# A CIN tower on one core: one-hot products turned round, and tile 1's gathers held until they are done

## The reference, cut to what matters

```python
e = jnp.stack([tbl_0[ids[:, 0]], ..., tbl_23[ids[:, 23]]], axis=1)   # 1024 x 24 x 16
for W in Ws:                                                         # three layers, 64 maps each
    Wr = W.reshape(24, H_prev, 64)
    Xk = jnp.einsum('bfd,bhd,fho->bod', X0, Xk, Wr)
    outs.append(Xk.sum(axis=2))
h = jnp.concatenate([z, dense_ctx], axis=1)
h = jnp.maximum(h @ W_top1 + b_top1, 0.0)
h = jnp.maximum(h @ W_top2 + b_top2, 0.0)
y = h @ W_top3
```

## Time and profile before

| what | value |
|---|---|
| median of 3 runs (lowest, highest) | 413.58 us (409.85, 417.03) |
| the profiled execution, in all | 417.16 us |
| its span, first to last instruction | 415.3 us |
| PE / VectorE / ScalarE / POOL busy | 87% / 73% / 44% / 56% of the span |
| mean granted TensorE clock | 0.992 |

### The profile page before, as it was taken

One profiled execution on the slowest core, in us unless ns is written; L12 is line 12 of the kernel. 1 busy time (PEld: TensorE's weight loads), 2 busy tenths in 40 slices (PEclk: granted clock), 3 DMA queues, 4 the chain that ended last, 5 costly groups with the idle time before them and its releaser, 6 DMA issues.

```text
span 415.3 us, 6926 instructions
## 1 busy us (share of the span) xinstructions
PE 363.0 (87%) x2624; PEld 161.1 (39%) x2624; DVE 302.4 (73%) x299; ACT 184.6 (44%) x347; POOL 231.3 (56%) x324
## 2 busy tenths in 40 slices
PE   1531485999999999898999999999899999999997
PEld 0200372523323333344343434444343354443465
DVE  3210452599698989859798989989799999898700
ACT  1000110024362426444756566565457475745374
POOL 5777106888888888888878888888830000000000
PEclk9999998899999999999999999999999999999999
DMA  7520047969988798998799989997999899941000
GB/s 217 154 42 6 2 96 170 243 134 230 209 214 208 178 242 153 235 243 196 155 227 244 240 162 228 257 253 145 234 252 261 156 238 239 225 117 36 2 1 4
DMA packets 56884, 71.07 MB, mean 171 GB/s; under 512 B 31153, under 2 KB 36017, under 8 KB 56850
## 3 DMA queue, kind: packets, MB, share of 16 engines
q1 hardware_dynamic: 49138, 69.04, 71.7%
q0 software_dynamic: 5632, 1.45, 3.4%
q10 hardware_dynamic: 2080, 0.13, 0.3%
HBM read 50.15 MB, written 1.58 MB: 125 GB/s over the span
## 4 chain that ended last, share of the span: by engine, by line
PE 80%; issue 9%; DMA 4%; ACT 3%; DVE 2%; another core or an unknown queue 2%; SPq 0%; DVEq 0%; ACTq 0%
PE ps_x L406 48%; PE ps_b L406 12%; PE ps_tower L406 9%; PE ps_turn L406 6%; PE ps_turn L459 2%; DMA x_scratch<-x_rows 1%; PE ps_turn L467 1%; DMA small_ids_sb<-small_ids 1%; DVE Z L383 1%; DMA C<-x_scratch 1%; PE ps_tower L412 1%; DVE Z L373 1%; ACT x_diag L691 1%; ACT C L665 0%
## 5 line engine op out<-in xcount | busy, mean ns | idle before, releaser
L383 DVE TENSOR_TENSOR Z<-A,ps_b 128x1024 f32<-128x1024 f32 x192 | 221.8, 1213 | 18.9 <-PE ps_x L406 13.6
L215 POOL DMA_INDIRECT x_rows<-tbl,ids_sb x176 | 180.4, 1025 | 52.7 <-issue 23.9
L406 PE MATMUL ps_x<-Z,w_sb 128*64 128x512 f32 x768 | 184.9, 598 | 0.9 <-DVE Z L383 0.5
L406 PEld LDWEIGHTS ps_x<-Z,w_sb 128*64 128x64 f32 x768 | 49.4, 136 | 80.8 <-issue 58.9
L373 DVE TENSOR_TENSOR Z<-A,C 128x1024 f32<-128x1024 f32 x48 | 57.4, 1222 | 30.5 <-DMA C<-x_scratch 10.4
L227 POOL MEMSET pause_sb<- 128x288 f32 x144 | 50.7, 352 | 21.4 <-DMA x_scratch<-x_rows 21.3
L691 ACT ACTIVATE x_diag<-ps_turn,mask_sb 128x192 f32<-128x192 f32 x128 | 50.6, 605 | 12.2 <-PE ps_turn L467 11.6
L406 PE MATMUL ps_b<-Z,small_sb 128*16 128x128 f32 x288 | 21.1, 357 | 34.7 <-issue 25.2
L406 PE MATMUL ps_x<-Z,w0s_sb 128*64 128x512 f32 x192 | 46.3, 608 | 5.5 <-DVE Z L373 5.3
L704 ACT COPY G<-ps_turn 128x416 f32<-128x416 f32 x31 | 15.7, 506 | 61.4 <-PE ps_turn L406 42.8
L674 ACT COPY ps_b<-B_sb 128x1024 f32<-128x1024 f32 x36 | 37.1, 1030 | 0.0
(11 more groups left out here) (60 smaller groups left out, 192.7 us busy)
## 6 DMA issues: line engine op xcount, KB each, us to landing
A<-x_scratch SPq DMA_DIRECT2D x48, 512.0 KB
B_sb<-x_sb SPq DMA_DIRECT2D x72, 256.0 KB
C<-x_scratch SPq DMA_DIRECT2D x32, 512.0 KB
x_rows<-tbl,ids_sb POOLq DMA_INDIRECT x176
x_quarters<-x_scratch SPq DMA_DIRECT2D x16, 96.0 KB
x_scratch<-x_rows SPq DMA_DIRECT2D x7, 192.0 KB
small_ids_sb<-small_ids SPq DMA_DIRECT2D x2, 512.0 KB, 5.2
w_sb<-w SPq DMA_DIRECT2D x2, 384.0 KB
```

What stands on the lines that cost most here:

```text
L215: pool.indirect_dma_start(out=x0_rows[t % 2][:, f * D:(f + 1) * D], out_offset=None, in_=tables[f], in_offset=bass.IndirectOffsetOnAxis(ap ...
L383: nc.vector.tensor_tensor(Z[s % ZR][:, :], A[u % AS][i][:, :], ps_b[j % 2][:, :], ALU.mult)\
L406: return nc.tensor.matmul(out, lhsT, rhs, start=start, stop=stop)
```

## The change

In the products the operands change places: the ones (128 x 128) are held in the array and the table's chunk (128 x 16) streams. A product's result is then one sample a partition and 16 numbers wide, so the eight tables of a set stand side by side in the first 128 columns of one bank of `ps_b`, and ScalarE copies them straight into `x0_rows`. `x0_small`, its two memsets, its eight copies and the four transposes go. All products of a set are one accumulation in that bank: the first clears it, the last ends it. The wait for the identity moves behind the products. POOL waits, between tile 0's eight gathers and tile 1's 24, until all 18 chunks have been used.

```diff
@@ POOL
             for f in range(FR):
                 gather(0, f, first_gathered)
+            pool.wait_ge(hot_used, len(HOT))
             for t in range(1, TILES):
@@ VectorE
-            for k in range(SETS):
-                nc.vector.memset(x0_small[k][:, :], 0.0).then_inc(small_ids_ready, 1)
             dve.wait_ge(small_rows_in, 16)
...
-                    dve.wait_ge(small_ids_ready, SETS + k + 1)
+                    dve.wait_ge(small_ids_ready, k + 1)
@@ TensorE
-            def turn_small(k):
-                pe.wait_ge(ident_in, 16)
-                pe.wait_ge(small_copied, 4 * (k + 1))
-                for half in range(2):
-                    last = nc.tensor.transpose((ps_turn, ps_x2)[k][:, TILE_ROWS * half:TILE_ROWS * (half + 1)],
-                                               x0_small[k][:, TILE_ROWS * half:TILE_ROWS * (half + 1)], id_sb[:, :])
-                last.then_inc(small_turned, 1)
...
                 pe.wait_ge(hot_ready, n + 1)
                 for f in range(FR):
-                    g, half = f % 4, f // 4
-                    last = mm(ps_b[k][32 * g:32 * g + D, 512 * half:512 * half + TILE_ROWS], small_sb[:, n, f, :],
-                              Z[n % ZR][0:CR, TILE_ROWS * f:TILE_ROWS * (f + 1)], c == 0, c == chunks[k] - 1)
+
+                    last = mm(ps_b[k][:, D * f:D * (f + 1)], Z[n % ZR][0:CR, TILE_ROWS * f:TILE_ROWS * (f + 1)],
+                              small_sb[:, n, f, :], (c, f) == (0, 0), (c, f) == (chunks[k] - 1, FR - 1))
                 last.then_inc(hot_used, 1)
-                if c == 2 and k > 0:
-                    turn_small(0)
-            turn_small(SETS - 1)
+            pe.wait_ge(ident_in, 16)
             keep_warm(WARM[0])
@@ ScalarE
-            act.wait_ge(small_ids_ready, SETS)
             for k in range(SETS):
                 act.wait_ge(hot_used, sum(chunks[:k + 1]))
-                for g in range(4):
-                    nc.scalar.copy(x0_small[k][32 * g:32 * g + D, :].rearrange("p (h b) -> p h b", h=2),
-                                   ps_b[k][32 * g:32 * g + D, :].rearrange("p (h b) -> p h b", h=2)[:, :, 0:TILE_ROWS])\
-                        .then_inc(small_copied, 1)
-                act.wait_ge(small_turned, k + 1)
-                nc.scalar.copy(x0_rows[0][:, FR * D * (k + 1):FR * D * (k + 2)].rearrange("p (f d) -> p f d", d=D),
-                               (ps_turn, ps_x2)[k][:, 0:2 * TILE_ROWS].rearrange("p (f e) -> p f e", e=32)[:, :, 0:D])\
+                nc.scalar.copy(x0_rows[0][:, FR * D * (k + 1):FR * D * (k + 2)], ps_b[k][:, 0:FR * D])\
                     .then_inc(small_ready, 1)
```

More of the change, by code:

```diff
@@ L95, in cin_tower @@
         small_ids_f32 = [sb(f"small_ids_f32_{k}", [CR, FR * TILE_ROWS]) for k in range(SETS)]
-        x0_small = [sb(f"x0_small{k}", [128, 2 * TILE_ROWS]) for k in range(SETS)]
         pause_sb = sb("pause_sb", [128, PAUSE])
@@ L157, in cin_tower @@
         paused = sem("paused")
-        hot_used, small_turned = sem("hot_used"), sem("small_turned")
+        hot_used = sem("hot_used")
         z_used, b_made, x2_turned, x0_turned, g_summed = (sem(n) for n in (
@@ L164, in cin_tower @@
             "z3_summed", "h1_summed", "h2_summed", "y_summed"))
-        small_copied, small_ready = sem("small_copied"), sem("small_ready")
+        small_ready = sem("small_ready")
         c_copied, b_copied = sem("c_copied"), sem("b_copied")
```

## The result

The changed kernel takes 459.8 us, the median of four runs (446.12 to 470.18), beside 413.05 us (409.85 to 417.03). The ratio is 1.089 (95% interval 1.0702 to 1.1078); like every ratio here it compares fast runs alone, 446.12 us and a fifth run of 451.15 us with some 412 us, since the other three of the four (457.99 us and more) were slow runs. By the medians the kernel is slower by 47 us, by the ratio by 37 us, where the forecast had it 10 us faster, and both lie outside the range, which ended at 432 us.

The account below looks back on a forecast made before the run. Bound: a late, serial start behind slow one-hot products, then POOL's gather chain. Of 26 us gained at the start, 7.5 us slack plus 2.5 us earlier chain, 10 us, are kept: 417.16 to 407, from the median 404 us; range 400 to 432.

Parts of the forecast that it names:

- A pair of 128 + 16 is 64 ns fast and 131 ns slow.: Turned products on PE: weight load plus stream, costed per column at 0.44 ns fast and 0.91 ns slow.
- The slow pace for the first 4.7 us and the fast one for 252.: PE clock during the products: 36 pairs slow in 4.7 us, then 252 pairs fast in 16.1 us.
- rival 1: Products keep the slow pace, 288 x 131 ns, ending at 47 to 49 us; kernel 418 us; chance 0.22.
- Products end at 32 us.: End of the one-hot products on PE: 9.3 + 4.7 + 16.1 + 2 = 32 us, where they ended at 56.2.
- I take the slow stretch as gone: PE's sparse products from 14 to 47 us vanish once tile 1's gathers wait; 2 us remain for the first eight gathers.
- 2.4 us of copies and transposes go.: Between last product and store issue: 2.4 us before, about 0.6 us remaining, 1.8 us gained.
- It lands 6.1 us later: Tile 0's store, issued at 32.6 us, lands at 38.7 us, 26 us earlier than before.
- Tile 1's gathers take 30 us.: POOL: 24 gathers x 1.26 us from 32 us, leaving POOL free at 62.3 us against 64.79 before.
- Slack 7.5 us.: Tile 7's chain from last gather to use: 4 us before the use plus 3.5 us of SP held before the store.
- Rival 2: Gathers slow the keep-warm transposes and first cross product instead; gain 3 us, 410.5 us; chance 0.14.
- Rival 3: Slow stretch is not the gathers' doing; products end near 64 us, POOL stands still, kernel 436 us; chance 0.22.
- The rule of the Trainium skill: PE weight load takes columns divided by 1.2 in ns, 107 for 128; products would end near 46 us.

Follow-up runs that it names:

- the wide kernel: Changed kernel with each product streaming all eight tables, 128 columns instead of 16, into the same 128 columns; 428.14 us.
- the paced kernel: Kernel before with the 288-column pause memset before each of tile 1's gathers too; 396.66 us beside 415.69, later 395.6 us, ratio 1.0173.
- the fourth group: Runs without a crawl: kernel before 389.76 us, changed kernel 446.35, pause for tile 1 395.6, kernel before with the wait alone 397.69.

## Why the prediction was wrong, step by step

- *"A pair of 128 + 16 is 64 ns fast and 131 ns slow."* The step that failed. I split the transpose's 113 ns evenly over 256 columns. But load and stream overlap: the wide kernel's pair takes 111 ns at the fast clock with 128 streamed columns, a pair with 16 takes 103. The load alone sets the pair. Measured: 103 ns at 2.4 GHz, 212 ns at 1.2 GHz. The bound of 233 ns, the slow transpose, was the nearest row, and I took half of it.
- *"The slow pace for the first 4.7 us and the fast one for 252."* Failed too. The clock never rose in 61.6 us of pairs. I had seen it rise behind products of 128 streamed columns and carried that to 16. "A stream of pairs without a gap is as dense as PE gets", my argument against rival 1, is what the forced clock in the kernel with 40 more transposes refutes.
- *Products end at 32 us.* It should have been 9.3 + 288 x 0.213 = 70.6; measured 70.9. Of the 38.9 us of error 11.4 are the price of the pair (22 pairs in 4.7 us, then 266 x 0.103 us, and the 2 us for the gathers, would have ended at 43.4 us), and the other 27.5 the clock.
- *"I take the slow stretch as gone" beside the products.* Right: not one gap. But it was not gone from the kernel. With the old products the wait only moved it behind them.
- *2.4 us of copies and transposes go.* Right, or better: the store is issued 0.3 us behind the last product. *It lands 6.1 us later*: SP's load follows after 2.2 us here, and after 2.3 us in the kernel before where it doesn't crawl, but after 5.1 us in the paced kernel of the same group. What the longer ones wait for is not shown.
- *Tile 1's gathers take 30 us.* 33.3 us to the pause, since some take 1.9 us or more. POOL is free at 104.4 instead of 62.3 us: 38.9 + 3.2.
- *Slack 7.5 us.* Behind tile 2's first gather lay 349.8 us before, and 339.2 after: 10.6 us. My split of tile 7's chain came near it by luck: its 3.5 us for SP are 2.7 by the rows that it names (10.3 less 7.6), and the reason was another. These 10 us were no room in the transfers. In the kernel before, the crawl had made the compute late, and by these numbers the compute set the end, with 337.9 us behind the copy of x1, much as in four experiments where x1 comes late too (332.7 to 336.3 us); POOL's chain had the rest to spare. Where the crawl is missing, x1 is copied at 43.3 us, 339.0 us lie behind tile 2's first gather, and the slack is zero.
- *Rival 1* has the right mechanism (16 streamed columns may not raise the clock, or the load is slower than I cost it) and the wrong size, 131 for 212 ns: it put the end at 47 to 49 us and the time at 418. With the lateness that was measured, 39.6 us for tile 2's chain, less its 7.5 of slack, its sum gives 32 us on top of the profiled 417.16: 449.3 against 446.12 measured. *Rival 2* is what the wait alone does. *Rival 3* named the right rule ("a gap later than that costs POOL's chain its full length") and the wrong cause.
- *The rule of the Trainium skill* ("TensorE: Matmul & The Clock Gate", "LDWEIGHTS"), 107 ns for a load, I set aside because a pair with 128 more columns took 113. I had written the exception (the two overlap) and not given it a sum of its own. At the fast clock it holds (103 ns), and at the slow one the measured load takes twice that (212 ns).

The sum above is for the profiled execution. It took 446.12 us, no more than the fourth group's 444.54 to 448.13 us, where the changed kernel has no crawl: the 4.25 us steps at 102 to 107 us cost its end nothing that can be measured. Why three others of the median took 457.99 to 470.18 us is not shown, since none of them has a profile. In two other kernels with the wait, the one with 128 streamed columns and the one with 40 more transposes, 349.5 and 349.9 us lie behind tile 2's first gather where 339.2 do here, so some 10 us can be lost behind the wait. The kernel meant to take such a loss away, wait and pause together, ran in a group without the crawl.

**What stays open.** Why tile 1's gathers slow the issue of PE and VectorE in four groups of runs (that of the result is one) and not in two. By the times of the kernel before it is all or nothing within a group, the kernels and the data are the same, and one chip number has shown both. That the gathers bring it is shown (it comes, moves and goes with them); what else must be there is not. That PE ran short of instructions because their own loads were slowed was not tested.

## What to carry to other kernels

Before operands change places, price the pair by its dearer half: with 128 columns held and 16 streamed, the load is the whole price, and the clock that such a stream gets is to be read from a stream of the same shape, not from a dense one of another. A wait put in front of a long chain of one engine costs the end of whatever it waits for, so bound that end with the worst row, not with the middle. And a stretch in which no semaphore ends the waits should first be met by spreading what runs beside it: 0.35 us of pause before each gather gave 4.1% where the crawl was, at a cost of 1.7% where it wasn't; no version tried beat the kernel before in both.

## What the runs showed of the hardware that was not expected

- A gapless stream of 128-column loads with 16 streamed columns ran 61.6 us at 1.2 GHz without the clock rising, and lost a clock that had already risen. With 128 streamed columns the same loads went at the pace of 2.4 GHz from 13 us on.
- Load and product overlap almost in full for fp32 at 2.4 GHz: 111 ns for 128 + 128 against 103 for 128 + 16.
- Indirect gathers at one per 1.25 us can slow the issue of PE and VectorE to an instruction in 0.5 us and more, with idle or full DMA engines, and for 14 us beyond the last gather at that spacing (the kernel before with the wait: gathers to 55 us, crawl to 69). In three of the profiles with a crawl (the kernel before, it with the wait, and the changed kernel without it) the starts stand some 0.70 us or 2, 3 or 4 times that apart. At one per 1.57 us this all but went. In two groups of six it never showed.
